# Softmax attention re-tiled: fp32r row tiles, a ring of three maximum banks, maxima turned on VectorE

## The reference, cut to what matters

```python
x = layernorm(x + linear_attention(x))
h = layernorm(x, ln1_g, ln1_b)
q, k, v = (h @ Wq), (h @ Wk), (h @ Wv)              # 16 heads of 16
scores = einsum('bqhd,bkhd->bhqk', q, k) / sqrt(16)   # 4096 x 4096 for each head
attn = softmax(scores, axis=-1)
ctx = einsum('bhqk,bkhd->bqhd', attn, v).reshape(T, 256)
x = x + ctx @ Wo
x = x + mixture_of_experts(layernorm(x, ln2_g, ln2_b)); x = layernorm(x)
```

## Time and profile before

| | us |
|---|---|
| median of 3 runs (lowest, highest) | 4755.22 (4753.27, 4757.05) |
| the profiled execution: its own time | 4761.28 |
| its span, first to last instruction | 4759.5 |
| busy in the span: PE, ACT, DVE, POOL | 4242.6, 3703.6, 3624.0, 2061.3 |

### The profile page before, as it was taken

How to read it: one execution, slowest core, us unless ns; L and a number is a source line. 1 busy time by engine, 2 the same in 40 slices (tenths; PEclk the granted TensorE clock), 3 DMA queues, 4 the chain that set the end, 5 groups by cost and what they waited for, 6 DMA issues and landing times. The chain is left out here.

```text
span 4759.5 us, 95664 instructions
## 1 busy us (share of the span) xinstructions
PE 4242.6 (89%) x22137; PEld 1695.2 (36%) x22137; DVE 3624.0 (76%) x7256; ACT 3703.6 (78%) x6958; POOL 2061.3 (43%) x1018
## 2 busy tenths in 40 slices
PE   7569999999999999999999999999999973599990
PEld 4322222222222222222222222222222243499990
DVE  3658898989898989989898998889899863133335
ACT  1347999999999999999999999999999851255550
POOL 0011343434343443434343444434343423788875
PEclk8777999999999999999999999999999995799995
DMA  2231010101011010101010010101010004344333
GB/s 78 102 83 17 0 17 0 17 0 17 0 17 17 0 17 0 17 0 17 0 17 9 9 17 0 17 0 17 0 17 0 1 38 159 123 139 139 139 110 113
DMA packets 105462, 176.14 MB, mean 37 GB/s; under 512 B 16512, under 2 KB 87552, under 8 KB 99072
## 3 DMA queue, kind: packets, MB, share of 16 engines
q1 hardware_dynamic: 86864, 146.17, 11.9%
q0 software_dynamic: 6336, 16.79, 1.1%
q10 hardware_dynamic: 12144, 12.06, 0.7%
HBM read 117.55 MB, written 57.15 MB: 37 GB/s over the span
## 5 line engine op out<-in xcount | busy, mean ns | idle before, releaser
L741 ACT ACTIVATE probs<-s_ps 128x512 f32<-128x512 f32 x4096 | 2430.6, 601 | 212.9 <-PE s_ps L683 161.1
L590 POOL TENSOR_TENSOR probs_low<-probs 128x1024 f16<-128x1024 f32 x640 | 1324.2, 2070 | 2082.9 <-ACT probs L741 2082.9
L804 DVE TENSOR_TENSOR probs_low<-probs 128x1024 f16<-128x1024 f32 x1408 | 1820.4, 1295 | 20.9 <-ACT probs L741 20.7
L797 DVE CUSTOM_DVE_ANT_0 excess<-b_ps,excess 128x512 f32<-128x512 f32 x2048 | 1402.4, 687 | 332.6 <-ACT excess L728 265.6
L683 PE MATMUL s_ps<-q_ring,k_ring 98*128 (+1 forms) x4096 | 1565.3, 384 | 13.6 <-ACT probs L741 8.6
L728 ACT ACTIVATE excess<-diff_ps 128x512 f32<-128x512 f32 x2048 | 1215.3, 594 | 58.2 <-PE diff_ps L627 48.2
L666 PE MATMUL o_ps<-probs,v_parts 128*64 128x512 bf16 x4106 | 853.6, 412 | 74.6 <-ACT o_here L733 72.0
L683 PEld LDWEIGHTS s_ps<-q_ring,k_ring 98*128 98x128 bf16 x4096 | 434.3, 106 | 1159.9 <-ACT probs L741 571.7
L627 PE MATMUL diff_ps<-kd_ring,q_ring 96*128 (+1 forms) x2048 | 800.5, 391 | 50.9 <-issue 38.5
L636 PE MATMUL b_ps<-k_ring,q_ring 96*128 (+1 forms) x2048 | 797.9, 390 | 12.8 <-DVE unit_max L797 12.2
L666 PE MATMUL o_ps<-probs_low,v_parts 128*64 128x512 f16 x4106 | 783.5, 377 | 0.0
(11 more groups left out here) (195 smaller groups left out, 3434.9 us busy)
## 6 DMA issues: line engine op xcount, KB each, us to landing
w_in<-in_W SPq DMA_DIRECT2D x46, 1024.0 KB, 4.8
q_ring<-qs_dram SPq DMA_DIRECT2D x96, 128.0 KB, 4.4
k_ring<-ks_dram SPq DMA_DIRECT2D x96, 128.0 KB, 7.1
slots_dram<-zero_rows SPq DMA_DIRECT2D x24, 512.0 KB, 6.6
rows_e<-slots_dram SPq DMA_DIRECT2D x24, 512.0 KB, 3.9
y_slots_dram<-y_out ACTq DMA_DIRECT2D x23, 512.0 KB, 4.2
qs_dram<-parts SPq DMA_DIRECT2D x16, 384.0 KB, 2.9
ks_dram<-parts SPq DMA_DIRECT2D x16, 384.0 KB, 4.3
```

Source lines behind the costliest of these rows:

```text
L590: nc.gpsimd.tensor_tensor(probs_low[:, t % BUFS, :, :], probs[:, t % BUFS, :, :], high[:, :, :, 1], ALU.subtract).then_inc(pool_low_done, 1)
L741: nc.scalar.activation(probs[:, t % BUFS, k, :], s2_ps[:, k, :], ACT.Exp).then_inc(exp_done, 1)
L797: nc.vector.tensor_tensor_reduce(excess[:, u % 2, :], b_ps[:, u % 2, :], excess[:, u % 2, :], 1.0, LEAST, ALU.add, ALU.max, unit_max[:, u ...
L804: nc.vector.tensor_tensor(probs_low[:, t % BUFS, :, :], probs[:, t % BUFS, :, :], high[:, :, :, 1], ALU.subtract).then_inc(low_done, 1)
```

## The change

It replaces the whole of `softmax_attention` and adapts what stands around it.

- **Parts.** q and k are split into 2 fp32r parts, in 3 products: 48 rows instead of 96, and 50 with the two rows of maxima. Rows are held twice, at partitions 0 and 64 (TOP_ROW), keys 0 to 2047 at the one and 2048 to 4095 at the other. The stage before makes one part less: ACT's 5 copies and DVE's 5 subtractions of a chunk go. Two of the matmuls that stood one behind the other are now a pair on the upper and the lower rows of the array, in two banks.
- **Scores.** 16 slots (UNITS) of a pair; s_ps has two sets of two banks; ACT takes exp of both banks in one instruction of 1024 elements. probs is 16 units deep.
- **Probabilities.** DVE splits none. POOL splits 11 of the 16 units; the other 5 (FULL_UNITS) are not split: PE multiplies them in fp32 by v in fp32 (`v_full`), one matmul for each half of the array. SLOTS puts the 11 visits of values into slots up to 24, that is into the next chunk.
- **Maxima.** They are made 2 chunks ahead (LEAD) instead of 7. In each slot PE makes a pair of blocks (`max_pair`) ahead of the scores, into a ring of 3 banks (m_ps). In 5 slots (RELU_PAIRS) the pair is a difference and a block, with a Relu on ACT and the combined instruction on DVE, as before; in the other 11, DVE reduces both blocks by itself. A block waits until the block three before it has been read.
- **Turning the maxima** is now four small DVE operations (`finish_max`), one in each of slots 0 to 3, the last a 32x32 transpose, and then 16 small DMAs of SP for each chunk instead of 2.
- **Context.** One fp32 matmul turns o (`turn_o`, slot 11, into the ring), DVE copies 17 rows, and SP stores them and the sums unscaled to DRAM. Queries are read chunk by chunk: 6 DMAs each (`load_q`), 9 for each head's keys.
- **Output projection.** It loads the context turned already, spreads 1/z over the rows of a head by a matmul, scales on DVE, and multiplies by Wo, with two sets of banks, chunks written out.

The diff, cut to its core, with 8 spaces less ahead of each line:

```diff
-PARTS = 3
+PARTS = 2
+Q_PARTS = (0, 0, 1)
+K_PARTS = (0, 1, 0)
 SROWS = len(Q_PARTS) * DH
 MROWS = 2
 AROWS = SROWS + MROWS
...
+Q_BUFS = 4
+LEAD = 2
...
+FULL_UNITS = (3, 6, 9, 12, 15)
+POOL_UNITS = tuple(t for t in range(UNITS) if t not in FULL_UNITS)
+VISITS = ((0, 1), (3,), (2, 4), (6,), (5, 7), (9,), (8, 10), (12,), (11, 13), (15,), (14,))
+SLOTS = (10, 12, 14, 15, 16, 18, 19, 20, 22, 23, 24)
+COPY_SLOT, TURN_SLOT = 8, 11
+RELU_PAIRS = (1, 4, 7, 10, 14)
+FINISH_SLOTS = (0, 1, 2, 3)
+RING_BLOCKS = 2 * UNITS + 1
+TURN_BLOCK = 2 * TURN_SLOT + 2
+SPLIT_OPS = 5 + len(FULL_UNITS)
...
+def block_of(t, k):
+    return 2 * t + k + (1 if t > TURN_SLOT else 0)
...
-        for s in range(5):
-            act.wait_ge(rest_ready, c * 5 + (s + 6))
-            nc.scalar.activation(parts[:, b, s, 1, :], rest[:, s, :], ACT.Copy).then_inc(mid_ready, 1)
...
-        for s in range(5):
-            dve.wait_ge(mid_ready, c * 5 + (s + 1))
-            nc.vector.tensor_tensor(parts[:, b, s, 2, :], rest[:, s, :], parts[:, b, s, 1, :], ALU.subtract
-                                    ).then_inc(low_ready, 1)
...
-probs = sb("probs", [P, BUFS, STEP // P, CHUNK])
-probs_low = sb("probs_low", [P, BUFS, STEP // P, CHUNK], F16)
...
-s2_ps = ps("s2_ps", [P, STEP // P, CHUNK])
-diff_ps = ps("diff_ps", [P, 2, CHUNK])
-b_ps = ps("b_ps", [P, 2, CHUNK])
...
+q_stage = sb("q_stage", [TOP_ROW + AROWS, Q_BUFS * CHUNK], F32R)
+k_ring = sb("k_ring", [TOP_ROW + AROWS, 2, SIDE], F32R)
+kd_ring = sb("kd_ring", [SROWS, 2, SIDE], F32R)
...
+v_full = sb("v_full", [P, 2, len(FULL_UNITS), 2, V_COLS])
...
+probs = sb("probs", [P, UNITS, 2, CHUNK])
+probs_low = sb("probs_low", [P, len(POOL_UNITS), 2, CHUNK], F16)
...
+s_ps = ps("s_ps", [P, 2, 2, CHUNK])
+m_ps = ps("m_ps", [P, 3, CHUNK])
 o_ps = ps("o_ps", [P, CHUNK])
...
+    def rows(n, buf):
+        sp.wait_ge(max_ready, n + 1)
+        for at in (0, TOP_ROW):
+            for r in range(MROWS):
+                row = q_stage[at + SROWS + r:at + SROWS + r + 1, ds(buf * CHUNK, CHUNK)].bitcast(F32)
+                row = row.rearrange("a (t b n) -> a t b n", t=TPC, b=P // SQ)
+                for b in range(P // SQ):
+                    sp.dma_start(row[:, :, b, :], max_turned[SQ * b:SQ * b + TPC, r, :]).then_inc(rows_in, 16)
...
+        i = sp.snap(h * CHUNKS + qc)
+        if loads:
+            sp.wait_ge(s_done, i * UNITS + 1)
+            n = qc + LEAD + 1
+            load_q(sp.snap(h + n // CHUNKS), n % CHUNKS, n % Q_BUFS)
+            if more and qc == 0:
+                load_head(sp.snap(h + 1), sp.snap((h + 1) & 1))
+        if ahead:
+            rows(i + 1, (qc + 1) % Q_BUFS)
+        if before:
+            store(i - 1, 1 - qc % 2, sp.snap(h - 1) if qc == 0 else h, (qc - 1) % CHUNKS)
...
+        for t in POOL_UNITS:
+            pool.wait_ge(exp_done, i * UNITS + (t + 1))
+            nc.gpsimd.tensor_tensor(probs_low[:, POOL_UNITS.index(t), :, :], probs[:, t, :, :],
+                                    high_view[:, t, :, :, 1], ALU.subtract).then_inc(pool_low_done, 1)
...
+    def max_pair(it, c, t):
+        par, buf = c % PAIR // CHUNKS, c % Q_BUFS
+        col = buf * CHUNK + P * (t // KCH)
+        key = CHUNK * (t % KCH)
+        for k, at in enumerate((0, TOP_ROW)):
+            b = block_of(t, k)
+            if c * RING_BLOCKS + b > 2:
+                pe.wait_ge(m_read, it * (PAIR * RING_BLOCKS) + (c * RING_BLOCKS + b - 2))
+            ring = kd_ring if k == 0 and t in RELU_PAIRS else k_ring
+            nc.tensor.matmul(m_ps[:, b % 3, :], q_stage[at:at + SROWS, col:col + P],
+                             ring[at:at + SROWS, par, key:key + CHUNK], start=True, stop=True).then_inc(m_done, 1)
+    def scores(it, c, t):
+        par, buf = c % PAIR // CHUNKS, c % Q_BUFS
+        if c * UNITS + t > 1:
+            pe.wait_ge(exp_done, it * (PAIR * UNITS) + (c * UNITS + t - 1))
+        for k, at in enumerate((0, TOP_ROW)):
+            last = nc.tensor.matmul(s_ps[:, t % 2, k, :], k_ring[at:at + AROWS, par, P * t:P * t + P],
+                                    q_stage[at:at + AROWS, buf * CHUNK:buf * CHUNK + CHUNK], start=True, stop=True)
+        last.then_inc(s_done, 1)
+    def values(it, c, visit):
...
+        for t in VISITS[visit]:
+            if t in POOL_UNITS:
+                pe.wait_ge(pool_low_done, i * len(POOL_UNITS) + (POOL_UNITS.index(t) + 1))
+            first, final = t == VISITS[0][0], t == VISITS[-1][-1]
+            if t in FULL_UNITS:
+                for k in range(2):
+                    last = nc.tensor.matmul(o_ps[V_COLS * k:V_COLS * k + V_COLS, :],
+                                            v_full[:, par, FULL_UNITS.index(t), k, :], probs[:, t, k, :],
+                                            start=False, stop=False)
+                continue
+            for n, part in enumerate((high_view[:, t, :, :, 1], probs_low[:, POOL_UNITS.index(t), :, :])):
+                for k in range(2):
+                    last = nc.tensor.matmul(o_ps[V_COLS * k:V_COLS * k + V_COLS, :],
+                                            v_parts[:, par, first_tile(t) + 2 * k, :], part[:, k, :],
+                                            start=(first and n == 0), stop=(final and n == 1))
         last.then_inc(pv_done, 1)
...
+        nc.tensor.matmul(m_ps[:, TURN_BLOCK % 3, :], gather[:, :], o_here[:, :], start=True, stop=True
+                         ).then_inc(o_turned, 1)
...
+        pe.wait_ge(rows_in, (it * PAIR + (c + 1)) * ROW_DMAS)
+        for t in range(UNITS):
+            if ahead:
+                max_pair(it, c + LEAD, t)
+            scores(it, c, t)
+            for visit, slot in enumerate(SLOTS):
+                if slot == t:
+                    values(it, c, visit)
+                if slot == t + UNITS and c > 0:
+                    values(it, c - 1, visit)
+            if t == TURN_SLOT and c > 0:
+                turn_o(it, c)
...
+    def excess_pair(n, t):
+        act.wait_ge(m_done, n * (2 * UNITS) + (2 * t + 1))
+        nc.scalar.activation(excess[:, :], m_ps[:, block_of(t, 0) % 3, :], ACT.Relu).then_inc(excess_ready, 1)
...
+            if ahead and t in RELU_PAIRS:
+                excess_pair(i + LEAD, t)
+            act.wait_ge(s_done, i * UNITS + (t + 1))
+            if not first:
+                act.wait_ge(pv_done, i * len(VISITS) + (visit_of(t) + 1 - len(VISITS)))
+            nc.scalar.activation(probs[:, t, :, :], s_ps[:, t % 2, :, :], ACT.Exp).then_inc(exp_done, 1)
+            if t == COPY_SLOT and not first:
+                copy_o(i)
...
+    def pair(n, t, b, skip):
+        qt, j = t // KCH, t % KCH
+        if t in RELU_PAIRS:
+            dve.wait_ge(excess_ready, n * len(RELU_PAIRS) + (RELU_PAIRS.index(t) + 1))
+            dve.wait_ge(m_done, n * (2 * UNITS) + (2 * t + 2))
+            dve.sem_inc(dve_passed, 1)
+            nc.vector.tensor_tensor_reduce(excess[:, :], m_ps[:, block_of(t, 1) % 3, :], excess[:, :], 1.0, LEAST,
+                                           ALU.add, ALU.max, unit_max[:, b, qt, 2 * j:2 * j + 1]
+                                           ).then_inc(m_read, 2)
+            return
+        for k in range(2):
+            dve.wait_ge(m_done, n * (2 * UNITS) + (2 * t + k + 1))
+            nc.vector.tensor_reduce(unit_max[:, b, qt, 2 * j + k:2 * j + k + 1], m_ps[:, block_of(t, k) % 3, :],
+                                    AX.X, ALU.max).then_inc(m_read, 1 + skip * k)
+        nc.vector.tensor_scalar(ctx_stage[:, b, :], m_ps[0:O_COLS, TURN_BLOCK % 3, :], 1.0, None, ALU.mult
+                                ).then_inc(m_read, 1)
...
+        if step == 0:
+            dve.wait_ge(m_read, n * RING_BLOCKS + RING_BLOCKS)
+            nc.vector.tensor_reduce(tile_max[:, :], unit_max[:, b, :, :], AX.X, ALU.max).then_inc(tile_max_done, 1)
+        if step == 1:
+            dve.wait_ge(tile_max_done, n + 1)
+            nc.vector.scalar_tensor_tensor(max_parts[:, 0, 0:TPC], tile_max[:, :], -1.0, no_max[:, :],
+                                           ALU.mult, ALU.add).then_inc(high_done, 1)
+        if step == 2:
+            dve.wait_ge(high_done, n + 1)
+            nc.vector.scalar_tensor_tensor(max_parts[:, 1, 0:TPC], tile_max[:, :], -1.0,
+                                           max_parts[:, 0, 0:TPC].bitcast(F32), ALU.mult, ALU.subtract
+                                           ).then_inc(low_done, 1)
+        if step == 3:
+            dve.wait_ge(low_done, n + 1)
+            nc.vector.transpose(max_turned[:, :, :].rearrange("p r n -> p (r n)"),
+                                max_parts[:, :, :].bitcast(F32).rearrange("p r n -> p (r n)")).then_inc(max_ready, 1)
...
-        att_ps = banks[:, 2:4, :].rearrange("p b (t d) -> p (b t) d", t=2)
...
+    def spread(c):
...
+        for j in range(HALVES):
+            heads = of_head[:, c, HEADS // 2 * j:HEADS // 2 * j + HEADS // 2, :].rearrange("p h d -> p (h d)")
```

(5 more changed lines are left out.)

649 lines of the change are left out of this document (284 added, 365 removed).

## The result

The changed kernel takes 4771.24 us (median of 11 runs, 4765.11 to 4779.53) where the kernel before takes 4754.81 beside it: ratio 1.0037, 95% interval 1.0027 to 1.0046. It is 0.4% slower; I had forecast 7% faster. Its profiled execution has a span of 4773.4 us, 13.9 more than before.

What follows compares the result with a forecast made beforehand. It took TensorE's issue order and its bank exchange with ScalarE as the bound, closely followed by ScalarE. From 4759.5 us, main stretch -247, maxima alone -69, projection -6 and splits -3 gave 4434, about 4430; range 4080 to 4850.

Steps and rivals of the forecast that it cites:

- The chunk of 24.9 us: Main attention stretch: the 16 slots of a chunk, walked along the ring, sum to 24.9 us against 27.1 before.
- W: TensorE's own work in a slot, said to decide eight slots: 1.10 to 1.57 us each, 11.8 a chunk.
- the Relu chain: Matmul, ScalarE's Relu, VectorE's combined instruction, bank release: 1.97 us; Relu slots 1, 4, 7, 10, 14 together 9.8.
- rival 2: Values in unsplit units: fp32 matmul pairs run one behind the other, 28.2 us a chunk, 4850 us; chance 0.12.
- the slots without either: Slots 5, 9 and 13 of a chunk: 0.78 and twice 1.25 us, together 3.3.
- Maxima alone: Stretch before the main attention: 2 chunks for 7, 34 us for 103.3, 69 less; perhaps 10 more at half clock.
- Start: Constants, v splits and loads before the first stage's work, 23.1 us: no change.
- projection: Output projection, 65.2 us before: 6 us less, between 20 less and 10 more.
- SP: 16 small row DMAs a chunk, 10.7 us, landed by 19 us, before the next chunk's scores need them at 24.9.
- 1, GpSimd's pace: Main stretch: if the Relu chain hides, GpSimd's 22.1 us sets the chunk, 4080 us; chance 0.18.
- 3: TensorE pairs: row tiles don't overlap (4920 us) or weight loads are exposed behind matmuls (4880); chance 0.08.
- 4: Row DMAs over 0.95 us each (4790 at 1.2), or TensorE partly at 1.2 GHz (past 5500); chance 0.07 with the like.

Runs made afterwards that it cites:

- e7: e1 with the first unit's values between maximum and score pairs in the five two-unit slots, two more tiling changes in each: 4735.13 us, 0.9955.
- e1: Changed kernel with no Relu pairs, so VectorE reduces all 32 maximum blocks of a chunk: 4468.22 us, 0.9388.
- e3: Changed kernel, but a block taking a Relu block's bank waits only for the Relu, not for VectorE's combined instruction: 4502.68 us, 0.9461.
- e2: Changed kernel with TensorE's loop over pairs of heads written out, so without a jump back: 4737.37 us, 0.9950.
- e9: Changed kernel with GpSimd subtracting only half of the columns, its instructions about half as long: 4772.12 us, 1.0025.
- e14: Changed kernel with only the edit of e13 to VectorE's two small operations on the maxima: 4776.78 us, 1.0031.
- e6: e5 with TensorE's loop written out: 4382.55 us, 0.9207.
- e10: e6 with GpSimd subtracting only half of the columns, as in e9: 4303.86 us, 0.9042.
- e11: e6 with VectorE's four small operations on the maxima in slots 0, 3, 4, 6 instead of 0 to 3: 4661.98 us, 0.9783.
- e13: e12 with two small maxima operations given one SBUF tensor in, the second split into four of one column: 4346.38 us, 0.9133.
- e17: e13 with the first small operation still 128x4 wide, but taking a scalar by partition (a column of zeros): 4346.00 us, 0.9128.
- e16: e13 with the first small operation also split into four of one column, with a scalar by partition: 4343.51 us, 0.9121.
- e12: e6 with one Relu pair back, in slot 12, its bank freed by the Relu: 4360.90 us, 0.9160.
- e4: Changed kernel with the values spread evenly over the slots, the five Relu pairs kept: 4839.50 us, 1.0164.
- e5: Changed kernel with no Relu pairs and the values spread evenly over the slots: 4407.71 us, 0.9260.

## Why the prediction was wrong, point by point

**The chunk of 24.9 us is the step that failed.** The mechanism was right (the ring walked slot by slot, W or the Relu chain ending last), and the sign hung on its sizes. A chunk takes 27.1 + 65 / 126 = 27.6. The break-even that I had named in rival 2, 27.7, is itself wrong: it took 27.1 for every chunk before, but seven took 22.0, so it is (3436.4 + 78 - 52) / 126 = 27.5. The kernel stands just above it. The forecast stood 2.6 us below, on a sum of 16 latencies. Of the 343 us by which the main stretch is longer than forecast, W holds some 150, the Relu chain some 120, the slots without either 10, and the passages of the loop and the clock 65; the other stages together give 4 back.

- *W* (the slots that TensorE's own work sets). Predicted 1.54, 1.50, 1.10; measured 1.67, 1.68, 1.23. I took 0.09 for each change of tiling from the earlier trace rows, where a bf16 matmul over the whole array stands ahead of the values and `turn_o` behind them. Out of the values into fp32r row tiles, the first pair is 0.50 long and the next start is 0.33 to 0.34 away instead of 0.23: 0.11 more in each of 11 visits; e7 shows the price of 0.31 for two changes. Full units needed 1.01 to the next pair where I had 0.95. The eight slots set by W: 13.0 for 11.8.
- *The Relu chain.* Predicted 1.97, measured 2.15: 0.50 for the matmul, which stands behind a change, not 0.38, and 0.26 to DVE, not 0.18. With slots 10 and 14, 10.8 for 9.8. e1 and e3 show what the whole chain costs: 309 and 274 us (1.0037 less 0.9388 and 0.9461, of 4760). That this comes near the 341 us by which the forecast was off is chance: most of that cost was in the forecast, and only some 120 us of the error are the chain's.
- *Slots without either.* 3.4 for 3.3. ACT's start every 0.95 and DVE's pair in 1.22 (1.28 here) did no harm.
- *Passages of the loop and the clock.* In no term: 65 us. I had looked at TensorE's clock only for a rival with all of the time at half clock, and not at what a jump back costs in a loop with 16 chunks written out, nor at short falls of the clock behind waits; e2 gives 41 us back.

**The other terms.** Maxima alone 43 us for 34, at a granted clock of 0.50, the "perhaps 10 more" that I had set beside the sum. Start 4.0 less for 0; projection 13.2 less for 6. SP: 16 transfers in 9.86 us for 10.7, issued by some 17 us into the chunk, and not waited for. GpSimd is busy 78% of the main stretch (2743.6 of 3532.5), not the 85 to 90% that I had named as a sign of being right.

**The rivals.** 1, GpSimd's pace: no, e9. Its condition, a chain that hides, was made true by e1, and the chunk fell to 25.0, not 22.1, since TensorE's visits and the ring's 1.28 came next. 2 and 3: both pairs overlap. 4: no wait for rows; of the clock a small part is true: 0.98 in the main stretch, and some 48 us of slots at 1.2 GHz. Two sums in the rivals are off by their own walk, without weight here: an fp32 pair of 1.55 gives 27.3 a chunk, and loads exposed give 28.0 and 4820, not 4880.

**A sentence that was false.** I wrote that no VectorE instruction with two SBUF inputs is left. The two of `finish_max` are such: 128x4 elements, which I had counted within 0.5 us for four small operations, with no wait for GpSimd. In the changed kernel that costs nothing (e9, e14), because the slots concerned are set by other chains; in e6 it costs some 0.5 us a chunk (e10), in e11 far more. The Trainium skill (GPSIMD Engine Reference, Specifications) says what I had cited it for, and adds VectorE's modes with two ports. By the Trainium skill (VectorE: DVE Perf Modes, What auto-detection actually checks) such a mode, 2x_2P, is taken when a single source and the destination are in SBUF and their outermost non-unit dimensions are both even or equal. As far as they go the traces agree: 128x4 with two inputs waits, 128x4 with one input does too (e13, e17), and reductions of 512 columns that read PSUM don't (668 to 693 ns in all 2816). A single column has no such dimension, and the page does not name the case; here it doesn't wait (e16, at most 216 ns).

**A version that beats both.** e16: values spread evenly, one Relu whose bank ScalarE frees, TensorE's loop written out, small operations in columns: 4343.5 us, 8.8% less than the kernel before. e6, e12 and e13 lie on the way to it.

## What to carry to other kernels

When engines hand banks round in a ring, cost the longest chain of each slot from rows that have the same operation behind the same neighbour; here errors of 0.02 to 0.3 us in each of 16 slots, with 65 us of gaps and low clock, were the whole gain. Before spending a chain of three engines to spare one of them 0.6 us of work, look who waits for its end: freeing the bank one step earlier, or leaving the detour out, was worth 6%. An even spread pays only once the longest slots are set by what is spread (e4 lost 1.3% by the edit that won 1.3% in e5).

## What was not expected of the hardware

- An fp32r pair of row tiles behind bf16 or fp32 column tiles lasts 0.50 us instead of 0.39 and holds the next start back by 0.10; a round trip into the values and out costs some 0.3.
- A VectorE operation on 128x4 elements in SBUF lasts until the GpSimd instruction beside it ends: 0.15 us alone, up to 1.67.
- Where TensorE's loop of 16 written-out chunks jumps back, it stands for 2.2 to 2.7 us, and the granted clock of the 20 us behind it is 0.66 to 0.87.
- TensorE's granted clock also fell to 0.50 for about 3 us behind waits of 1.2 us (slot 1 of the changed kernel, 14 chunks) and of 0.64 and 0.44 us in two slots running (e11); a chunk mostly lost 1.5 us by it.
